# A four-layer residual kernel on TensorE: attention in eight places of the array, and a new order of the step

## The chip, the cores and the metric

The kernel runs on one core of one Trainium2 chip. The metric is the device time of one execution in microseconds (us). TensorE does the matrix products and turns (transposes), VectorE, ScalarE and GpSimd work elementwise, and SyncE issues the transfers. Inputs lie in device memory, tiles in SBUF, results of TensorE in eight PSUM banks of 512 fp32 columns.

## The reference

`x` has 64 sequences of 64 tokens of 512 values, fp32. Four layers follow each other, each added to its input:

```python
x = x + L0(x)   # x @ W.T + (x @ A[idx0].T) @ Bm[idx0].T * scal[idx0], rank 16, one of 8 adapters per sequence
x = x + L1(x)   # per sequence: weights[idx1].T (64x64) @ x (64x512), one of 200 matrices
x = x + L2(x)   # causal attention, 16 heads of 32, q scaled by min(cond, 4), scores / sqrt(32), then Wo
x = x + L3(x)   # as L1, with another table of 8 matrices and idx3
```

## The kernel before, in words

The 64 sequences go in 16 steps of four (256 tokens, two tiles of 128 tokens, two sequences in a tile). Every dense product with a 512x512 matrix is made from operands split in a high and a low part (`*_hi`, `*_lo`, type fp32r): high by high, high by low, low by high. Such a product is 24 matmuls of 512 columns a step (layer 0, values, output of attention) or 48 of 256 columns (keys, queries). The small products are plain fp32: mixing (layers 1 and 3, `mix`, L417, four matmuls in the four 64x64 quarters of the array), scores (L466) and attention (L485). In the trace an fp32 matmul of these three has two records, each with a weight load of its own; a turn has one.

Scores and attention use block-diagonal operands: `place_k`, `place_q`, `place_v` (L243, L249, L254) copy keys, queries and values out of PSUM into tiles with zeros in them, so that a 128x128 matmul makes the scores of two heads and two sequences at once, of which the zeros throw away the cross terms. `beta` scales the scores on VectorE (L802). Softmax goes: mask and maximum (VectorE), minus the maximum (GpSimd), exp (ScalarE), sum and reciprocal (VectorE), times the reciprocal (GpSimd for tile 0, VectorE for tile 1), then the turn of the probabilities on TensorE (L477).

The order on each engine is written out by hand in a function `step`, and engines meet through semaphores (`wait_ge`). TensorE's step i (L524) is: turn x of step i+1, queries, values of tile 0, scores, values of tile 1, the adapters' first product and layer 0 of step i+1, turns of the probabilities with the last of layer 0 between them, attention, the adapters' second product (`adapters_up`, L409), the output product of tile 0, layer 1 of step i+1, the output product of tile 1 with the turns of x1 inside it, keys of step i+1 with layer 3 of step i inside them. The low part of the adapters' intermediate (`xa_lo_part`, L771) has to be in place before `adapters_up`. SyncE's step (L328) gathers the per-sequence matrices, loads x two steps ahead and stores y. Before the loop the five 512x512 matrices are loaded one behind another on SyncE's queue, turned and split.

## Time and profile before

| | before |
|---|---|
| time of three runs, us | 713.11, 714.54, 714.82 (median 714.54) |
| the profiled execution: time, span, us | 714.74, 713.2 |
| busy: TensorE, VectorE, ScalarE, GpSimd | 96%, 53%, 45%, 16% |
| mean granted clock of TensorE | 0.988 |

The span runs from the first to the last instruction, the time is 1.5 us longer. "Busy" counts instructions in execution. Each duration of a matmul record holds a latency that overlaps its neighbours, so TensorE's rate is read from the starts of records, not from their durations. "PE" is TensorE, "PEld" its weight loads, "DVE" VectorE, "ACT" ScalarE, "POOL" GpSimd, "SPq" SyncE's queue, "L472" line 472.

### The profile page before, as it was taken

The page shows a single profiled execution, that of the slowest core. Times are in us where ns is not written, and L with a number is a line of the kernel's source. Part 1 is how long each engine was busy: PE and PEld are TensorE (multiplying, and loading weights), DVE is VectorE, ACT ScalarE, POOL GpSimd, SP SyncE. Part 2 cuts the span into 40 slices and gives each one's busy share as a digit, 9 for nine tenths or more (in the row PEclk, how much of TensorE's full clock was granted, in tenths as well). Part 3 has the DMA queues.
Part 4 walks back from the last instruction along what each step waited for, and adds up shares of the span by engine and source line. Part 5 has one row for each costly group of instructions (what it writes and reads, how often), then busy time and mean ns, then how long its engine had stood idle before and what let it go on. Part 6 is the DMA issues. An engine that isn't in the chain of part 4 may idle for free.

```text
span 713.2 us, 14872 instructions
## 1 busy us (share of the span) xinstructions
PE 683.2 (96%) x5240; PEld 584.7 (82%) x5240; DVE 378.9 (53%) x565; ACT 319.9 (45%) x648; POOL 113.9 (16%) x98
## 2 busy tenths in 40 slices
PE   5699999999999999999999999999999999999986
PEld 4489797888979798797979879797987979798774
DVE  3645555464555646455564645546463554636362
ACT  3544355443535544353554435354543535444342
POOL 4003012030301203030120303002030300303030
PEclk9979999999999999999999999999999999999998
DMA  6520111102011010201101020110202011020000
GB/s 185 191 94 8 53 37 35 49 4 81 7 52 37 33 52 4 81 7 52 37 30 54 5 81 7 52 37 18 65 5 81 7 52 37 9 75 4 29 1 30
DMA packets 32768, 31.68 MB, mean 44 GB/s; under 512 B 18550, under 2 KB 18550, under 8 KB 32758
## 3 DMA queue, kind: packets, MB, share of 16 engines
q1 hardware_dynamic: 32758, 31.55, 14.2%
q8 instruction: 6, 0.10, 0.1%
q14 instruction: 4, 0.03, 0.0%
HBM read 22.61 MB, written 8.91 MB: 44 GB/s over the span
## 4 chain that ended last, share of the span: by engine, by line
PE 92%; DMA 2%; DVE 2%; SPq 1%; issue 1%; ACT 0%; POOL 0%; ACTq 0%; DVEq 0%
PE banks L374 13%; PE banks L375 12%; PE banks L376 12%; PE banks L504 9%; PE banks L472 8%; PE banks L493 5%; PE banks L421 5%; PE banks L512 4%; PE banks L481 4%; PE banks L404 4%; PE banks L402 4%; PE banks L406 4%; PE banks L436 2%; PE banks L395 2%; PE banks L385 2%; PE banks L414 2%
## 5 line engine op out<-in xcount | busy, mean ns | idle before, releaser
L374 PE MATMUL banks<-x1T_hi,w_hi 128*128 128x256 f32 x512 | 148.3, 290 | 0.0
L375 PE MATMUL banks<-x1T_lo,w_hi 128*128 128x256 f32 x512 | 144.9, 283 | 0.0
L376 PE MATMUL banks<-x1T_hi,w_lo 128*128 128x256 f32 x512 | 144.8, 283 | 0.0
L374 PEld LDWEIGHTS banks<-x1T_hi,w_hi 128*128 128x128 f32 x512 | 98.1, 192 | 15.3 <-issue 15.3
L375 PEld LDWEIGHTS banks<-x1T_lo,w_hi 128*128 128x128 f32 x512 | 98.1, 192 | 0.0
L376 PEld LDWEIGHTS banks<-x1T_hi,w_lo 128*128 128x128 f32 x512 | 98.0, 191 | 0.0
L742 DVE COPY k_bd<-banks 32x512 f32<-32x512 f32 x64 | 44.2, 691 | 98.9 <-PE banks L376 98.2
L907 POOL TENSOR_TENSOR w_own<-w_in,own 128x128 f32<-128x128 f32 x32 | 14.7, 460 | 492.7 <-PE banks L421 287.0
L922 POOL TENSOR_TENSOR probs<-probs,row_max 128x1024 f32<-128x1024 f32 x32 | 61.0, 1907 | 84.2 <-DVE row_max L808 84.2
L677 ACT ACTIVATE probs<-probs 128x1024 f32<-128x1024 f32 x32 | 34.0, 1061 | 72.2 <-POOL probs L922 71.9
L802 DVE SCALAR_TENSOR_TENSOR probs<-banks,beta,mask 128x512 f32<-128x512 f32 x64 | 46.4, 747 | 37.2 <-PE banks L472 36.6
L472 PEld LDWEIGHTS banks<-k_bd,q_bd 128*128 128x128 f32 x512 | 59.5, 192 | 2.9 <-issue 1.8
L472 PE MATMUL banks<-k_bd,q_bd 128*128 128x128 f32 x512 | 59.8, 275 | 1.6 <-DVE q_bd L742 1.6
L605 ACT ACTIVATE v_bd<-banks 64x256 f32<-64x256 f32 x128 | 48.6, 379 | 24.8 <-PE banks L376 23.3
L812 DVE TENSOR_REDUCE row_sum<-probs 128x16 f32<-128x1024 f32 x32 | 39.0, 1220 | 38.7 <-ACT probs L677 38.7
L605 ACT ACTIVATE y<-banks 128x512 f32<-128x512 f32 x32 | 17.4, 597 | 84.8 <-PE banks L421 84.8
L504 PE MATMUL banks<-w_hi,attnT_hi 128*128 128x512 f32 x128 | 54.9, 429 | 0.0
L605 ACT ACTIVATE k_bd<-banks 32x512 f32<-32x512 f32 x64 | 37.6, 588 | 35.3 <-PE banks L376 34.8
L402 PE MATMUL banks<-w_hi,xT_hi 128*128 128x512 f32 x128 | 51.5, 402 | 0.0
L374 PE MATMUL banks<-w_hi,x1T_hi 128*128 128x512 f32 x128 | 51.4, 401 | 0.0
L504 PE MATMUL banks<-w_lo,attnT_hi 128*128 128x512 f32 x128 | 50.4, 394 | 0.0
L375 PE MATMUL banks<-w_lo,x1T_hi 128*128 128x512 f32 x128 | 50.1, 391 | 0.0
(93 smaller groups left out, 1222.5 us busy)
## 6 DMA issues: line engine op xcount, KB each, us to landing
x_in<-in_x_dram SPq DMA_DIRECT2D x16, 512.0 KB, 3.7
out_dram<-y SPq DMA_DIRECT2D x16, 512.0 KB, 2.8
b_sel<-b_parts SPq DMA_DIRECT2D x192, 32.0 KB, 1.8
w_in<-in_L_cond_weights_dram SPq DMA_DIRECT2D x128, 16.0 KB
probsT<-in_L_cond_W_dram SPq DMA_DIRECT2D x1, 1024.0 KB, 6.1
probs<-in_L_cond_Wk_dram SPq DMA_DIRECT2D x1, 1024.0 KB, 7.7
x_both<-in_L_cond_Wq_dram SPq DMA_DIRECT2D x1, 1024.0 KB, 10.0
probsT<-in_L_cond_Wv_dram SPq DMA_DIRECT2D x1, 1024.0 KB, 12.1
```

Source lines behind the costliest of these rows:

```text
L374: nc.tensor.matmul(out_ap, s_hi, m_hi, start=(k == 0), stop=False)
L375: nc.tensor.matmul(out_ap, s_hi, m_lo, start=False, stop=False)
L376: last = nc.tensor.matmul(out_ap, s_lo, m_hi, start=False, stop=(k == n - 1))
L402: nc.tensor.matmul(bank[3 + t][:], xT_hi[:, c, tok(t)], w_hi[:, W0, c, :], start=(c == 0), stop=False)
L421: nc.tensor.matmul(bank[first_bank + t][half(r ^ t), :], w_own[half(r), t, :], rows_of[half(r), t, :], start=True, stop=True).then_inc(don ...
L472: last = nc.tensor.matmul(bank[b][:, hp % 4 * P:(hp % 4 + 1) * P], q_bd[:, t, hp, :], k_bd[:, t, hp, :], start=True, stop=True)
L504: nc.tensor.matmul(bank[5 + t][:], attnT_hi[:, c, tok(t)], m[:, WO, c, :], start=(c == 0 and m is w_hi), stop=False)
L605: return nc.scalar.activation(dst, src, ACT.Copy)
L742: return nc.vector.tensor_copy(dst, src)
L802: last = nc.vector.scalar_tensor_tensor(out=heads(probs[:, t, n * BANK:(n + 1) * BANK]), in0=heads(bank[(5 + 2 * t + n) % 8][:]), scalar=b ...
L812: nc.vector.tensor_reduce(row_sum[:, t, :], heads(probs[:, t, :]), AX.X, ALU.add).then_inc(sum_done, 1)
L922: nc.gpsimd.tensor_tensor(heads(probs[:, t, :]), heads(probs[:, t, :]), rows[:, t, :].unsqueeze(2).to_broadcast([P, HEADS, S]), op).then_i ...
```

## The change

It rewrites the step; the dense products, their number and their sizes stay as they are.

- Scores: `k_bd`, `q_bd` and their copies go. Keys are copied as they lie (`kT`), queries are scaled by `beta` on their way out of PSUM (`scale_q`). Each head of each sequence is one matmul of 32 rows, 64 stationary and 64 moving columns, in one of eight places of the array (four groups of 32 rows, two halves of columns): 64 matmuls a step in place of 16. The scores of a step are ready all at once.
- Attention: `v_bd` and its copies go. Each head of each sequence is one matmul of 64 rows, 32 stationary and 64 moving columns, again in eight places: 64 matmuls a step in place of 32.
- Order: step i begins with the scores of step i, then the output product of step i-1, the adapters' first product and layer 0 of step i+1, `adapters_up`, turns of the probabilities around layer 3 of step i-1, layer 1 of step i+1, one tile's turn of x of step i+2, attention, the turns of x1 of step i+1, the other tile's turn of x, keys, queries, values of step i+1.
- The identity is added to the diagonal of W once, so x need not be added to layer 0's result; the copies of x0 and x1 are shared between ScalarE and VectorE; the copy `keep_x1` goes from ScalarE to GpSimd. x0 and y have tiles of their own.
- In the preparation the five matrices are loaded on ScalarE's queue, each to a buffer of its own; queries and values of step 0 are made before the loop; Wv is turned behind `adapters_up(0)` and Wo behind the queries.

```diff
-        k_bd = sb("k_bd", [P, TILES, HP, P])
...
+        qkT = sb("qkT", [P, 2, NC, PT])
+        qT = qkT[:, 0]
+        kT = qkT[:, 1]
+        v = sb("v", [P, TILES, D])
...
+        def in_steps(engine, step):
+            step(0)
+            with engine.Fori(1, LAST_ALIKE + 1) as i:
+                step(i)
+            for i in range(LAST_ALIKE + 1, PAIRS):
+                step(i)
...
+            def step(i):
+                if after(i, 2):
+                    gather_own_b(i + 2)
+                if after(i, -1):
+                    store_y(i - 1)
+                if after(i, 3):
+                    turned_in(i + 3)
+                if after(i, 1):
...
         @block.tensor
...
+            def scores(i):
+                pe.wait_ge(k_copied_act, i + 1)
+                pe.wait_ge(k_copied_dve, i + 1)
+                pe.wait_ge(q_scaled, TILES * (i + 1))
+                for mm in range(NC // 2):
+                    for t in range(TILES):
+                        for r in range(SEQT):
+                            for h in range(2):
+                                for j in range(JG):
+                                    m, rows = 2 * mm + h, slice(j * HD, (j + 1) * HD)
+                                    last = nc.tensor.matmul(bank[SC[j]][half(h), key_columns(m, t, r)],
+                                                            qT[rows, m, own_tokens(t, r)],
+                                                            kT[rows, m, own_tokens(t, r)], start=True, stop=True)
+                last.then_inc(s_mm, 1)
...
+            def attend():
+                for t in range(TILES):
+                    for m in range(NC):
+                        for r in range(SEQT):
+                            for j in range(JG):
+                                at = j % 2 * BANK + (m // 2 * TILES + t) * P + m % 2 * S
+                                head = (JG * m + j) * HD
+                                last = nc.tensor.matmul(
+                                    attn_bank(r)[j * HD:(j + 1) * HD, m, t, :], v[half(r), t, head:head + HD],
+                                    probsT[half(r), j // 2, at:at + S], start=True, stop=True)
+                last.then_inc(av_mm, 1)
...
-                for hp in range(HP):
-                    b = (5 + 2 * t + hp // 4) % 8
-                    last = nc.tensor.matmul(bank[b][:, hp % 4 * P:(hp % 4 + 1) * P], q_bd[:, t, hp, :],
-                                            k_bd[:, t, hp, :], start=True, stop=True)
-                    if hp % 4 == 3:
-                        last.then_inc(s_mm, 1)
...
-                for hp in range(HP):
-                    for b in range(SEQT):
-                        at = hp * P + b * S
-                        last = nc.tensor.matmul(
-                            bank[1 + t][half(hp % 2), hp // 2 * P + b * S:hp // 2 * P + (b + 1) * S],
-                            v_bd[:, t, b, hp, :], probsT[:, t, at:at + S], start=True, stop=True)
-                last.then_inc(av_mm, 1)
...
-            def step(i, more=True):
-                if more:
-                    turn_x(i + 1)
-                queries(i)
-                if more:
-                    values(0)
-                scores(i, 0)
-                if more:
-                    pe.wait_ge(xT_split, TILES * (i + 2))
-                scores(i, 1)
-                if not more:
-                    values(0)
-                values(1)
-                if more:
...
+            def step(i):
+                prev, nxt, nxt2 = after(i, -1), after(i, 1), after(i, 2)
+                scores(i)
+                if prev:
+                    for t in range(TILES):
+                        layer2_out(i - 1, t)
+                if nxt:
+                    if prev:
+                        pe.wait_ge(x2_added, TILES * (i - 1) + 1)
+                    else:
+                        pe.wait_ge(v_copied, 1)
                     adapters_down(i + 1)
-                    pe.wait_ge(v_placed, TILES * i + 1)
-                    layer0_dense(0)
-                    layer0_dense(1, range(NC - 1))
+                    layer0_dense()
+                    adapters_up(i + 1)
+                if prev:
+                    layer3_ready(i - 1)
+                if nxt:
+                    pe.wait_ge(xa_summed, i + 2)
                 turn_probs(i, 0)
-                if more:
-                    layer0_dense(1, [NC - 1])
+                if prev:
+                    layer3()
+                if nxt:
+                    layer1_ready(i + 1)
                 turn_probs(i, 1)
-                attend(i, 0)
-                if more:
-                    pe.wait_ge(xa_summed, i + 2)
-                attend(i, 1)
-                if more:
-                    adapters_up(i + 1)
-                layer2_out_hi(i, 0)
-                layer2_out_lo(i, 0, range(NC - 1))
-                if more:
-                    layer1_ready(i + 1)
-                layer2_out_lo(i, 0, [NC - 1])
-                if more:
+                if nxt:
                     layer1()
-                layer2_out_hi(i, 1, range(NC // 2))
-                if more:
-                    turn_x1(i + 1)
-                layer2_out_hi(i, 1, range(NC // 2, NC))
-                layer2_out_lo(i, 1)
-                if more:
-                    pe.wait_ge(x2_added, TILES * i + 1)
-                    keys(i + 1, [0])
-                layer3_ready(i)
-                if more:
-                    keys(i + 1, [1])
-                layer3()
-                if more:
-                    keys(i + 1, [2, 3])
...
+                pT_copied(i, HG)
+                if prev:
+                    pe.wait_ge(y_copied, TILES * i)
+                if nxt2:
+                    turn_x(i + 2, 0)
+                attend()
+                if nxt:
+                    turn_x1(i + 1, 0)
+                    turn_x1(i + 1, 1)
+                    if nxt2:
+                        turn_x(i + 2, 1)
+                    keys(i + 1)
+                    if nxt2:
+                        pe.wait_ge(xT_split, TILES * (i + 3))
+                    queries(i + 1)
+                    pe.wait_ge(attn_split, SEQT * (i + 1))
+                    values()
...
         @block.scalar
...
+            def step(i):
+                prev, nxt, nxt2 = after(i, -1), after(i, 1), after(i, 2)
+                if nxt:
                     select_a(i + 1)
...
+                    x0_copy(i + 1)
+                copy_pT(i, 0)
+                if prev:
+                    copy_y(i - 1)
+                copy_pT(i, 1)
+                if nxt:
                     x1_copy(i + 1)
                     x1T_hi_part(i + 1)
-                act.wait_ge(y_stored, 1 + 16 * i)
-                for t in range(TILES):
-                    act.wait_ge(y_mm, 1 + TILES * SEQT * i + SEQT * (t + 1))
-                    copy(y[:, t, :], bank[1 + t][:]).then_inc(y_copied, 1)
+                act.wait_ge(av_mm, i + 1)
+                copy(attn_of(attnT_hi[:], 0), attn_bank(0)).then_inc(attn_hi_done_act, 1)
+                if nxt2:
+                    for t in range(TILES):
+                        x_hi(i + 2, t)
+                if nxt:
+                    copy_k(i + 1)
+                    copy_v(i + 1)
...
         @block.vector
...
+            def scale_q(i):
+                for n in range(2):
+                    dve.wait_ge(q_mm, 2 * i + n + 1)
+                    nc.vector.tensor_tensor(
+                        qT[:, 2 * n:2 * n + 2, :].rearrange("p m (q s) -> p m q s", s=S),
+                        bank[SC[n]].rearrange("p (m q s) -> p m q s", m=2, s=S),
+                        beta[:, bass.ds(i * PSEQ, PSEQ)].unsqueeze(1).unsqueeze(3)
+                        .to_broadcast([P, 2, PSEQ, S]), ALU.mult).then_inc(q_scaled, 1)
...
+            def step(i):
+                prev, nxt, nxt2 = after(i, -1), after(i, 1), after(i, 2)
+                for g in range(HG):
+                    mask_and_max(i, g)
+                    if prev:
+                        add_x1(i - 1, g)
                 sums(i, 0)
+                if nxt:
+                    sum_xa(i + 1)
+                    scale_xa(i + 1)
                 sums(i, 1)
-                for t in range(TILES):
-                    dve.wait_ge(pT_mm, TILES * i + t + 1)
-                    copy(probsT[:, t, BANK:2 * BANK], bank[(6 + 2 * t) % 8][:]).then_inc(pT_copied_dve, 1)
-                    if more and t == 0:
-                        sum_xa(i + 1)
-                        scale_xa(i + 1)
-                if more:
+                if nxt:
                     xa_lo_part(i + 1)
-                for t in range(TILES):
-                    dve.wait_ge(attn_hi_done, TILES * i + t + 1)
-                    rest(attnT_lo[:, :, tok(t)], bank[1 + t][:].rearrange("p (c n) -> p c n", n=P),
-                         attnT_hi[:, :, tok(t)]).then_inc(attn_split, 1)
-                if more:
-                    add_x(i + 1)
-                add_x1(i, 0)
-                if more:
+                    x0_copy(i + 1)
+                for g in range(HG):
+                    copy_pT(i, g)
+                if nxt:
+                    x1_copy(i + 1)
                     x1T_lo_part(i + 1)
-                add_x1(i, 1)
+                dve.wait_ge(av_mm, i + 1)
+                copy(attn_of(attnT_hi[:], 1), attn_bank(1)).then_inc(attn_hi_done_dve, 1)
+                for r, done in enumerate((attn_hi_done_act, attn_hi_done_dve)):
+                    dve.wait_ge(done, i + 1)
+                    rest(attn_of(attnT_lo[:], r), attn_bank(r), attn_of(attnT_hi[:], r)).then_inc(attn_split, 1)
+                if nxt2:
+                    x_lo(i + 2)
+                if nxt:
+                    copy_k(i + 1)
+                    scale_q(i + 1)
...
         @block.gpsimd
...
+            def step(i):
+                for g in range(HG):
+                    pool.wait_ge(s_max, HG * i + g + 1)
+                    with_rows(ALU.subtract, g, row_max, s_less_max)
+                pool.wait_ge(inv_done, HG * i + 1)
+                keeps_x1(i)
+                with_rows(ALU.mult, 0, row_inv, probs_done[0])
+                keep_x1()
                 build_w3(i)
-                if more:
-                    build_w1(i + 1)
-                for t in range(TILES):
-                    pool.wait_ge(s_max, TILES * i + t + 1)
-                    with_rows(ALU.subtract, t, row_max, s_less_max)
-                pool.wait_ge(inv_done, TILES * i + 1)
-                with_rows(ALU.mult, 0, row_inv, probs_done[0])
+                if after(i, 2):
+                    build_w1(i + 2)
```

## Rows read from the trace of the kernel before

**Rows 1.** The page: span, busy time, share and instructions of each engine.

```profile
span 713.2 us, 14872 instructions
...
PE 683.2 (96%) x5240; PEld 584.7 (82%) x5240; DVE 378.9 (53%) x565; ACT 319.9 (45%) x648; POOL 113.9 (16%) x98
```

**Rows 2.** Window of one whole step (time, busy time by engine, clock, DMA).

```profile
351.76:393.49 41.73, 41.46 (x325) 35.55 (x324) 22.53 (x33) 19.10 (x39) 6.78 (x6) 1.00 0.12 38
```

**Rows 3.** Timeline of TensorE, one step's queries, values, scores: start, duration (us).

```profile
343.46 0.28 PE L374 MATMUL banks<-x1T_hi,w_hi 128*128 128x256 f32 x1
...
348.85 0.40 PE L374 MATMUL banks<-w_hi,x1T_hi 128*128 128x512 f32 x1
...
351.60 3.73 PE L472 MATMUL banks<-k_bd,q_bd 128*128 128x128 f32 x32
```

**Rows 4.** Chain that ended last, same step: start, length (us), what.

```profile
363.82 0.87 PE banks L481 x8
...
366.25 2.06 PE banks L493 x64
368.32 0.27 issue
368.59 0.70 PE banks L414 x2
...
372.24 1.02 PE banks L421 x8
```

**Rows 5.** Timeline at the start of a mixing product, window to 338.26.

```profile
338.23 0.15 PEld L421 LDWEIGHTS banks<-probs,w_own 64*64 64x64 f32 x4
338.24 0.66 PE L421 MATMUL banks<-probs,w_own 64*64 64x512 f32 x4
```

**Rows 6.** Windows near the end and of the preparation, columns as Rows 2.

```profile
35.90:44.20 8.30, 7.20 (x33) 5.58 (x34) 3.00 (x6) 4.08 (x7) 0.46 (x1) 0.50 0.48 157
...
697.72:700.85 3.13, 3.13 (x66) 3.06 (x65) 1.19 (x2) 1.19 (x2) 0.00 (x0) 0.63 0.00 0
```

**Rows 7.** Chain near the end: the last scores, softmax and attention.

```profile
681.88 0.13 PE banks L376
...
697.72 3.12 PE banks L493 x64
```

**Rows 8.** Groups of VectorE in one step: busy us, mean ns.

```profile
L802 DVE SCALAR_TENSOR_TENSOR probs<-banks,beta,mask 128x512 f32<-128x512 f32 x4 | 2.9, 746 | 2.4 <-PE banks L472 2.4
...
L808 DVE TENSOR_REDUCE row_max<-probs 128x16 f32<-128x1024 f32 x2 | 2.4, 1220 | 0.1
...
L796 DVE TENSOR_TENSOR probs<-banks,x_both 128x512 f32<-128x512 f32 x2 | 1.4, 692 | 1.2 <-PE banks L512 1.2
...
L817 DVE TENSOR_TENSOR probs<-probs,row_inv 128x1024 f32<-128x1024 f32 x1 | 1.2, 1228 | 0.0
L746 DVE TENSOR_TENSOR xa_parts<-xa,xa_hi 32x128 fp32r<-32x128 f32 x2 | 0.6, 282 | 0.2 <-ACT xa_hi L605 0.2
L814 DVE RECIPROCAL row_inv<-row_sum 128x16 f32<-128x16 f32 x2 | 0.5, 253 | 0.1
...
L761 DVE TENSOR_TENSOR xa_sum<-banks,xa_low 64x256 f32<-64x256 f32 x1 | 0.4, 406 | 0.0
```

**Rows 9.** Groups of ScalarE in the same step.

```profile
L677 ACT ACTIVATE probs<-probs 128x1024 f32<-128x1024 f32 x2 | 2.1, 1061 | 4.3 <-POOL probs L922 4.3
...
L605 ACT ACTIVATE x1T_hi<-banks 128x512 fp32r<-128x512 f32 x2 | 1.1, 596 | 0.5 <-PE banks L436 0.5
```

**Rows 10.** Groups of GpSimd in the same step.

```profile
L922 POOL TENSOR_TENSOR probs<-probs,row_max 128x1024 f32<-128x1024 f32 x2 | 3.8, 1906 | 4.3 <-DVE row_max L808 4.3
```

**Rows 11.** Timeline of TensorE in the preparation, waits in brackets.

```profile
34.16 1.02 PE L414 MATMUL banks<-b_sel,xa_parts 96*128 96x512 f32 x2 [3.51 <-DMA b_sel<-b_parts]
36.23 1.99 PE L421 MATMUL banks<-y,w_own 64*64 64x512 f32 x8 [1.04 <-DVE y L784]
...
40.72 3.62 PE L362 MATMUL banks<-ident,probs 128*128 128x128 f32 x16
```

More of the change, by code:

```diff
@@ new lines, in gather, with gather_b @@
+            def gather(dst, table, at, arrived, moved):
+                for n in range(PSEQ):
+                    t, b = divmod(n, SEQT)
+                    sp.dma_start(dst[half(b ^ t if moved else b), t, :],
+                                 table[bass.ds(at[n], 1), :, :].rearrange("a c e -> (a c) e")).then_inc(arrived, 16)
+            def gather_b(at):
+                for n in range(PSEQ):
+                    t, b = divmod(n, SEQT)
+                    for k, part in enumerate((0, 0, 1)):
+                        row = (k * SEQT + b) * RANK
+                        sp.dma_start(b_sel[row:row + RANK, t, :].bitcast(F32),
+                                     b_parts[part, bass.ds(at[n] * RANK, RANK), :]).then_inc(b_loaded, 16)
@@ new lines, in project_T @@
+            def project_T(w, out_banks, m, split=None):
+                out_ap = bank[out_banks[m // 2]][:, (m % 2) * PT:(m % 2 + 1) * PT]
+                cols = slice(m * P, (m + 1) * P)
+                for c in range(NC):
+                    nc.tensor.matmul(out_ap, w_hi[:, w, c, cols], x1T_hi[:, c, :], start=(c == 0), stop=False)
+                    nc.tensor.matmul(out_ap, w_lo[:, w, c, cols], x1T_hi[:, c, :], start=False, stop=False)
+                if split is not None:
+                    pe.wait_ge(x1_split, split)
+                for c in range(NC):
+                    last = nc.tensor.matmul(out_ap, w_hi[:, w, c, cols], x1T_lo[:, c, :], start=False,
+                                            stop=(c == NC - 1))
+                return last
@@ new lines, in keys, with queries, values @@
+            def keys(i):
+                pe.wait_ge(x1_hi_done, TILES * (i + 1))
+                for m in range(NC):
+                    last = project_T(WK, MIX, m, split=TILES * (i + 1) if m == 0 else None)
+                    if m % 2 == 1:
+                        last.then_inc(k_mm, 1)
+            def queries(i):
+                for m in range(NC):
+                    last = project_T(WQ, SC, m)
+                    if m % 2 == 1:
+                        last.then_inc(q_mm, 1)
+            def values():
@@ L593, in _ @@
-            turn_x1(0)
-            turn_matrix(4, groups_of(4)[0])
-            keys(0, range(NC))
-            pe.wait_ge(turned_lo, GROUPS)
-            with pe.Fori(0, PAIRS - 1) as i:
-                step(i)
-            step(PAIRS - 1, more=False)
+            turn_x1(0, 0)
+            turn_x1(0, 1)
+            keys(0)
+            pe.wait_ge(xT_split, TILES * 2)
+            queries(0)
+            turn_matrix(WO)
+            pe.wait_ge(turned_lo, GROUPS_OF[WV][-1] + 1)
+            values()
@@ L602, in _ @@
+            pe.wait_ge(turned_lo, GROUPS)
+            in_steps(pe, step)
+            for t in range(TILES):
+                layer2_out(PAIRS - 1, t)
+            layer3_ready(PAIRS - 1)
+            layer3()
         @block.scalar
@@ L952, in _ @@
                 nc.gpsimd.tensor_copy(mask[half(b), :], block_mask[half(b), half(b)]).then_inc(consts_step, 1)
[L953 to L954 removed]
+                pool.wait_ge(consts_step, 8 + 2 * b)
                 nc.gpsimd.tensor_copy(own[half(b), :], ident[half(b), half(b)]).then_inc(consts_step, 1)
[L956 to L958 removed]
+                pool.wait_ge(consts_step, 9 + 2 * b)
             build_w1(0)
[L960 to L962 removed]
+            build_w1(1)
+            in_steps(pool, step)
 _INS = ['x', 'itok_B_0_6', 'itok_B_1_198', 'cond_1', 'itok_B_0_7', 'L0_cond_W', 'L0_cond_A', 'L0_cond_Bm',
```

682 lines of the change are left out of this document (319 added, 363 removed).

## The prediction

> **What bounds the kernel.** I read the page first: TensorE is busy 96% of the span and no other engine much over half [rows 1]. Then a window of one whole step: 41.73 us, TensorE busy 41.46 of it at the full clock (1.00, 2.4 GHz), VectorE 22.5, ScalarE 19.1 [rows 2]. Each step in the middle takes this, so the kernel is TensorE's own rate, and a change is worth what it takes from TensorE's work or puts in as waits. Busy is not the rate, so I took the rate from starts. The 45 records of 256 columns between 343.46 and 348.85 follow each other at 0.120 us, the 12 of 512 columns between 348.85 and 351.60 at 0.229 [rows 3]; one of fp32 scores (16 matmuls of 128 columns, 32 records) takes 3.57/32 = 0.112, the scores ending near 355.17. One of attention (32 matmuls of 64 columns, 64 records) takes 2.06/64 = 32.2 ns [rows 4]. Last I read the chain at the end, where softmax has nothing to hide behind [rows 7], and the preparation [rows 11].
>
> **What stays.** Dense products, turns and mixings keep their number and sizes. In a step they are 96 records at 0.120 and 72 at 0.229, together 28.0; the adapters' first product 8 x 0.120 = 1.0 and the second about 0.5; 32 turns at 0.87 for eight, 3.5; two mixings at 1.02 [rows 4], 2.0. That is 35.0. With scores 3.57 and attention 2.06 it makes 40.7 of 41.73; the other 1.0 are the drains where the kind of product changes and one issue gap of 0.27 [rows 4]. The new order has about as many such changes, in fewer pieces: I take 1.0 again, the issue gap included. So the new step is 36.0 + S + A + new waits, S and A being the new scores and attention.
>
> **S and A, the disputed cost.** Each is 64 matmuls, so 128 records with weight loads, a record being 64 columns long, in eight places. Before shows no such stream; nothing keeps a cost from being anywhere between the ends of the nearest rows. Upper end: the pair (weight load and matmul) of attention at 32.2 ns gives 128 x 32.2 = 4.1 us each. Lower end: at the start of a mixing, four pairs in four quarters begin within 338.23 to 338.26 [rows 5], about 6.7 ns a pair: 0.86 us each. In between decides what the 32.2 consists of. The two column halves of attention alternate, so one place has a record each 64 ns; and the last attention, where the clock is 0.63 of full [rows 6], takes 3.12/64 = 48.8 ns a record [rows 7]. If a record costs a + b with only b following the clock, then b(1/0.63 - 1) = 16.6, b = 28.3 and a = 3.9 ns. b is the array's time over two places; over eight it is 28.3/4 = 7.1. So 11 ns a pair, 1.4 us each for S and A. I take that, being worked out from the very stream nearest in shape, and keep 0.86 and 4.1 for the range.
>
> The Trainium skill speaks against the change here: TensorE: Matmul & The Clock Gate, section "Wait — 56ns, not 53.3ns?", says that starts of matmuls never come closer than about 25 ns, however few the columns. By it S and A would be 3.2 us each, an estimate from that page, and the kernel slower. The burst of four pairs in some 30 ns [rows 5] disagrees, but it is short; no row shows a long stream. The number does not enter the sum.
>
> The copies around them (`k_bd`, `q_bd`, `v_bd`) go from VectorE and ScalarE; those engines are hidden behind TensorE, so this is worth nothing by itself, only slack: VectorE's new step is about as long, 22 us of some 40. Adding the identity to W costs four small additions in the preparation and spares nothing on TensorE. The shared copies of x0 and x1 shorten a link by half of 1.2 us.
>
> **New waits, with t = 0 at the end of the scores.** TensorE: output product of step i-1 to 5.6, adapters' first product to 6.6, layer 0 to 12.1, then `adapters_up`. VectorE: mask and maximum of group 0, 2 x 0.69 + 1.22 [rows 8], to 2.8; `add_x1` waits for the first output product, to 3.6; group 1 to 6.2; `add_x1` to 6.9. GpSimd's subtraction takes 1.91 [rows 10], 2.8 to 4.7 and 6.2 to 8.15; exp 1.06 [rows 9], to 5.8 and 9.3. VectorE's sum 1.22 and reciprocal 0.25 [rows 8] of group 0 end at 8.4; GpSimd multiplies to 10.4. VectorE goes on with the adapters' sum and scale (two operations near 0.41 [rows 8]) to 9.3, sums of group 1 to 10.9, the multiplication 1.23 to 12.2, and only behind these, in its queue, `xa_lo_part`, 2 x 0.28 [rows 8], to 12.9. So `adapters_up` waits about 0.9: what is queued behind it is everything on TensorE. The probabilities, ready at 10.4 and 12.2, are then early. Next: copies of the turned probabilities against layer 1, about 0.15 late (ScalarE copies y between them). Attention is what covers the copies of x1. The keys wait for the second `x1T_hi`, 0.6 each [rows 9], less the 0.45 of the turn of x: 0.4. Queries' scaling and copies of keys and values end under the values and the scores. SyncE: 12 gathers for `b_sel` from 13.5, then y's store, the x tile after both its turns (21), w3 and w1; each is used at least 10 us later, and costs nothing. If that cover failed the x tile would hold the first turn of the next step. Waits together 1.5.
>
> Step: 36.0 + 1.5 + 2 x 1.4 = 40.3. Taking the order's fewer pieces as 0.4 saved (dense blocks no longer cut by turns and mixings) I arrive at 39.9, a gain of 1.8 a step, over 15 steps 27.5 us.
>
> **Once only.** In step 0 no output product covers softmax: `xa_lo_part` ends near 12 and layer 0 near 6.6, so 4.5 more than the steady wait, and some 1 at the halved clock, as after the idle time near the end [rows 6]. Preparation: before, `adapters_up(0)` starts at 34.16 after waiting for `b_sel` [rows 11]; now five matrices share the transfers with it: 0 to 2 us later. Wv's 16 turns, once hidden before that wait, come behind it at the halved clock, 3.4 us by those of Wo [rows 11, 6]; the addition to x gives 0.6 back: together +4. At the end scores, softmax and output products follow as before (31.3 us from 681.88 to the end of the span [rows 7, 1]), with output product and layer 3 of step 14 as cover in place of the values: -1. Sum: 713.2 - 27.5 + 5.5 + 4 - 1 = 694.2 of span, 1.5 more as time. That profiled execution took 714.74 against the median 714.54, so the median forecast is **695.5 us**.
>
> **Rivals.** (a) Issue bound: the small pairs don't come closer than in attention before, 32.2 ns each. S + A rise by 5.4, and sixteen steps make 695 + 87 = 782 us. By the 25 ns of that page of the Trainium skill the same rival would end near 753, an estimate. For it: no long stream of eight places is in the trace. Against: rows 5, and that 32.2 follows the clock [rows 6, 7]. It decides from about 15.7 ns a pair, where 19 us are eaten over 16 x 256 pairs; places that don't work side by side, the change not doing what it says, end here too. (b) Eight places at the burst's rate: S = A = 0.86, 17 us less, 678. For it the burst [rows 5]; against it the part of 3.9 ns. (c) Softmax's chain is later than I add up: VectorE's queue holds `xa_lo_part` behind group 1, and each link that comes 1 us late is 1 us a step. With 1.5 more, 695 + 23 = 718, even or a little slower. For it: one long queue order without slack at `adapters_up`. Against: before's durations repeat within 1%.
>
> **Chances.** Forecast (685 to 705) 0.50; (b) or between, 0.17; (a) in full 0.12, and in part (16 to 30 ns) 0.06; (c) 0.15, of which half still ends below 712. Faster by over 0.3% (about what a measurement of this kernel can tell from no change): 0.50 + 0.17 + 0.09 = 0.76. Within: 0.04. Slower: 0.20. The range from 674 to 726 leaves out (a) in full and part of the rest; the likeliest case's own range is 685 to 705.
>
> **What would show it.** Right: records of scores and attention at 9 to 14 ns from start to start, each block 1.2 to 1.8 us; a step of 39.5 to 40.5; one wait of about 1 us before `adapters_up` that VectorE's `xa_lo_part` ends; a wait near 5 us in step 0. Wrong: starts at 16 ns or more; blocks over 2 us; a wait for x, for turned probabilities or for `x1T_hi` over 1 us a step; a clock below 1.00 in the middle.

## The result and the profile after

The changed kernel takes 733.37 us (median of four runs, 732.72 to 736.07) against 714.68 before: a ratio of 1.0274, 95% interval 1.0244 to 1.0303. It is slower by 2.7%, and the time lies above the range of the prediction. The profiled execution has a span of 731.8 us, 18.6 more than before.

The page after (span, busy time, granted clock in 40 slices), beside [rows 1]:

```profile
span 731.8 us, 19651 instructions
...
PE 650.8 (89%) x7800; PEld 545.1 (74%) x7800; DVE 371.7 (51%) x537; ACT 224.6 (31%) x440; POOL 127.2 (17%) x111
...
PEclk9779999999999999999999999999999999999998
```

TensorE works 32 us less than before (650.8 against 683.2) and the span is longer: more than what was saved came back as waits, in the preparation and in each step. Who TensorE waits for, in total, times, longest (us):

```profile
PE banks L403 <- DVE xa_parts L758: 30.2, 15, 4.7
PE banks L403 <- DMA b_sel<-b_parts: 9.4, 1, 9.4
PE banks L362 <- DMA v<-in_L_cond_Bm_dram: 9.0, 1, 9.0
PE banks L373 <- DMA x_in<-in_x_dram: 7.7, 1, 7.7
PE banks L434 <- ACT x1T_hi L618: 5.6, 16, 0.7
```

The first row is a wait of every step, before the adapters' second product (now L403), for VectorE's low part. The next three are the preparation. The timeline of TensorE in a middle step answers to [rows 3, 4]:

```profile
341.23 0.70 PE L403 MATMUL banks<-b_sel,xa_parts 96*128 96x512 f32 x2 [1.83 <-DVE xa_parts L758]
...
346.39 1.48 PE L502 MATMUL banks<-probsT,v 64*32 64x64 f32 x128
347.80 1.09 PE L425 MATMUL banks<-ident,x_both 128*128 128x128 f32 x8
...
349.63 0.38 PE L434 MATMUL banks<-x1T_hi,w_hi 128*128 128x256 f32 x1 [0.30 <-ACT x1T_hi L618]
...
366.80 1.59 PE L477 MATMUL banks<-qkT 32*64 32x64 f32 x128
368.32 0.50 PE L517 MATMUL banks<-w_hi,attnT_hi 128*128 128x512 f32 x1
```

The scores go from 366.80 to 368.32, 1.52 us for 128 records where 3.57 stood; attention from 346.39 to 347.80, 1.41 us where 2.06 stood. That is 11.9 and 11.0 ns a record. The waits in brackets are 1.83 us before the adapters' second product and 0.30 before the keys. The chain gives the starts of the scores of several steps:

```profile
118.17 1.52 PE banks L477 x91
...
160.98 1.52 PE banks L477 x91
...
325.69 1.52 PE banks L477 x91
...
366.87 1.52 PE banks L477 x91
```

A middle step is 366.87 - 325.69 = 41.18 us, 0.55 less than the 41.73 of [rows 2]; the one from 118.17 to 160.98 is 42.81, and one more like it begins at 490.40. The first scores begin at 77 us. Before, the same amount of work stood at 59.66 (scores) plus 2.75 (the values of tile 1), 62.4 us. So the account is: preparation +14.5, the rest of the span (731.8 - 77 against 713.2 - 62.4) +4. The experiments below are called e1 to e11; there is no e5.

### The profile page after: what moved, and what is told of

Its sections match the earlier page's. It is cut to its first block, busy times and chain, and to the rows that moved or that the text cites. A ratio compares the mean times of both kernels' runs of the same rounds, so it can differ in the third digit from the quotient of the medians.

```text
span 731.8 us, 19651 instructions
## 1 busy us (share of the span) xinstructions
PE 650.8 (89%) x7800; PEld 545.1 (74%) x7800; DVE 371.7 (51%) x537; ACT 224.6 (31%) x440; POOL 127.2 (17%) x111
## 4 chain that ended last, share of the span: by engine, by line
PE 65%; DVE 17%; issue 8%; SPq 5%; ACT 2%; POOL 1%; DMA 1%; DVEq 0%; ACTq 0%; POOLq 0%
PE banks L434 9%; PE banks L439 8%; PE banks L435 8%; PE banks L411 5%; DVE row_sum L832 5%; PE banks L487 5%; DVE xa L777 4%; PE banks L459 4%; PE banks L461 4%; PE banks L463 4%; PE banks L477 3%; PE banks L502 3%; DVE probs L823 3%; PE banks L517 3%; PE banks L524 2%
## 5 line engine op out<-in xcount | busy, mean ns | idle before, releaser
L434 PE MATMUL banks<-x1T_hi,w_hi 128*128 128x256 f32 x512 | 129.9, 286 | 5.6 <-ACT x1T_hi L618 5.6
L823 DVE TENSOR_TENSOR probs<-banks,mask 128x512 f32<-128x512 f32 x64 | 41.1, 684 | 100.1 <-PE banks L477 100.1
L439 PE MATMUL banks<-x1T_lo,w_hi 128*128 128x256 f32 x512 | 82.3, 283 | 0.0
L618 ACT ACTIVATE v<-banks 128x512 f32<-128x512 f32 x32 | 19.1, 598 | 197.9 <-PE banks L463 197.9
L439 PEld LDWEIGHTS banks<-x1T_lo,w_hi 128*128 128x128 f32 x512 | 70.6, 192 | 0.0
L814 DVE TENSOR_TENSOR qkT<-banks,beta 128x512 f32<-128x512 f32 x32 | 22.1, 692 | 70.0 <-PE banks L439 70.0
L393 PE MATMUL banks<-w_lo,xT_hi 128*128 128x512 f32 x128 | 50.5, 394 | 0.0
L395 PE MATMUL banks<-w_hi,xT_lo 128*128 128x512 f32 x128 | 50.2, 392 | 0.0
L463 PE MATMUL banks<-w_hi,x1T_lo 128*128 128x512 f32 x128 | 49.8, 389 | 0.0
L487 PEld LDWEIGHTS banks<-ident,probs 128*128 128x128 f32 x256 | 31.9, 152 | 21.4 <-issue 19.5
L403 PE MATMUL banks<-b_sel,xa_parts 96*128 96x512 f32 x32 | 12.2, 464 | 39.6 <-DVE xa_parts L758 30.2
```

The costliest lines, as they stand in the source:

```text
L434: nc.tensor.matmul(out_ap, w_hi[:, w, c, cols], x1T_hi[:, c, :], start=(c == 0), stop=False)
L439: last = nc.tensor.matmul(out_ap, w_hi[:, w, c, cols], x1T_lo[:, c, :], start=False, stop=(c == NC - 1))
L463: last = nc.tensor.matmul(bank[OUT[t]][:], x1T_lo[:, c, tok(t)], w_hi[:, WV, c, :], start=False, stop=(c == NC - 1))
L487: last = nc.tensor.transpose(bank[SC[2 * g + n]][:, c * P:(c + 1) * P], probs[:, g, at:at + P], ident[:])
L823: last = nc.vector.tensor_tensor(heads(probs[:, g, n * BANK:(n + 1) * BANK]), heads(bank[SC[2 * g + n]]), mask[:].unsqueeze(1).to_broadcas ...
```

## The wait in each step

Why does VectorE come late? Its timeline in that step, and GpSimd's under it:

```profile
335.31 0.35 DVE L771 TENSOR_TENSOR xa_sum<-banks,xa_low 64x256 f32<-64x256 f32 x1
335.81 1.99 DVE L777 TENSOR_TENSOR xa<-xa_sum,scal_rows 64x256 f32<-64x256 f32 x1
337.73 1.20 DVE L832 TENSOR_REDUCE row_sum<-probs 128x16 f32<-128x1024 f32 x1
...
339.25 1.23 DVE L837 TENSOR_TENSOR probs<-probs,row_inv 128x1024 f32<-128x1024 f32 x1
340.51 0.58 DVE L758 TENSOR_TENSOR xa_parts<-xa,xa_hi 32x128 fp32r<-32x128 f32 x2
```

```profile
335.62 1.91 POOL L963 TENSOR_TENSOR probs<-probs,row_inv 128x1024 f32<-128x1024 f32 x1 [0.25 <-DVE row_inv L834]
337.47 1.24 POOL L973 COPY x_both<-x_both 128x1024 f32<-128x1024 f32 x1
```

The scaling of the adapters' intermediate (L777) took 0.42 us before, as one of the two operations of [rows 8] near 0.41; now it lasts 1.99. It starts 0.19 us behind GpSimd's multiplication of the probabilities and ends 0.27 behind its end. Before, it stood behind the turns of the probabilities, when GpSimd was idle. The Trainium skill, SBUF — State Buffer, section "Who interferes with whom", says that VectorE and GpSimd share a pair of ports, that a VectorE instruction with two SBUF inputs and a GpSimd instruction that reads SBUF contend for it, that one of them holds it for the whole instruction while the other stands still, and that a VectorE instruction with at most one SBUF input, outside the modes that use both ports, does not contend. The scaling has two SBUF inputs (`xa_sum`, `scal_rows`); the mask (L823), with one input from PSUM and one from SBUF, takes 1.28 us beside GpSimd's subtraction in this step and 1.29 beside nothing. Theory 1 is this hold. Theory 2 is that the scaling is slow in itself where it now stands, and that only its place in the queue counts.

**e1, the sum kept in PSUM.** The scaling then has one SBUF input. Nothing is moved; TensorE's turns of the probabilities wait for the scaling in place of the sum, since the sum's place in PSUM is read until then.

```diff
-                    pe.wait_ge(xa_summed, i + 2)
+                    pe.wait_ge(xa_scaled, i + 2)
...
-                nc.vector.tensor_tensor(xa_sum[:], bank[OUT[0]][half(0), 0:PT], xa_low[:], ALU.add)\
-                    .then_inc(xa_summed, 1)
+                here = bank[OUT[0]][half(0), 0:PT]
+                nc.vector.tensor_tensor(here, here, xa_low[:], ALU.add).then_inc(xa_summed, 1)
...
-                    xa[:].rearrange("p (b s) -> p b s", s=S), xa_sum[:].rearrange("p (b s) -> p b s", s=S),
+                    xa[:].rearrange("p (b s) -> p b s", s=S),
+                    bank[OUT[0]][half(0), 0:PT].rearrange("p (b s) -> p b s", s=S),
```

> The changed kernel with one edit: VectorE's sum of the adapters' intermediate stays in PSUM, so that the scaling behind it has one SBUF input in place of two; nothing else is moved. Theory 1 (VectorE's two-input operation stands still while GpSimd multiplies the probabilities): the scaling falls from 1.99 to about 0.42 us. The multiplication of group 1 by VectorE, also with two SBUF inputs, then meets GpSimd's copy of x1 and may start only at its end, so the wait before the adapters' second product shrinks by 0.5 to 0.6 us a step (1.2 if that copy does not hold it): 733.4 goes to 722 to 725 (716). Theory 2 (the scaling is slow for another reason, its position or its data): it stays near 2 us and the time within 0.3% of 733.4.

Measured: 717.41 us, 1.0065 of before (1.0041 to 1.0089), 16.0 less than after (the spans, 731.8 and 715.8, differ by as much): a step is 0.90 less, 14 of them 12.6, and the two long steps are gone, 3.2. It is less than the 722 to 725 expected. VectorE, then GpSimd:

```profile
328.98 0.40 DVE L772 TENSOR_TENSOR banks<-banks,xa_low 64x256 f32<-64x256 f32 x1
329.52 0.42 DVE L777 TENSOR_TENSOR xa<-banks,scal_rows 64x256 f32<-64x256 f32 x1
...
331.70 1.55 DVE L838 TENSOR_TENSOR probs<-probs,row_inv 128x1024 f32<-128x1024 f32 x1
```

```profile
329.28 1.91 POOL L964 TENSOR_TENSOR probs<-probs,row_inv 128x1024 f32<-128x1024 f32 x1 [0.25 <-DVE row_inv L835]
331.13 1.04 POOL L974 COPY x_both<-x_both 128x1024 f32<-128x1024 f32 x1
```

The scaling is back at 0.42 us in the midst of GpSimd's multiplication: Theory 1 holds, Theory 2 falls. The multiplication of group 1, with two SBUF inputs, begins while GpSimd copies x1 and takes 1.55 in place of 1.23, so that copy holds it too, by 0.3 us; I had expected 0.7. GpSimd pays as well: its copy lasts 1.04 here and 1.24 after, where it begins while the scaling still runs. A middle step is 40.28 us. The wait before the adapters' second product is 0.93 us a step (17.0 us in total less the 4.0 of step 0, over 14), the 0.9 that the prediction had.

**e2, the low part ahead of the multiplication.** Only the place in the queue changes.

```diff
                 nc.vector.reciprocal(row_inv[:, g, :], row_sum[:, g, :]).then_inc(inv_done, 1)
                 if g == 1:
+                    if after(i, 1):
+                        xa_lo_part(i + 1)
...
                 sums(i, 1)
                 if nxt:
-                    xa_lo_part(i + 1)
                     x0_copy(i + 1)
```

> The changed kernel with VectorE's low part of the adapters' intermediate placed ahead of its multiplication of group 1, the scaling left as it is. Theory 1 and the order in the queue: the scaling stays at 1.99 us, the low part is in place 1.3 us sooner, the wait before the adapters' second product shrinks from 1.8 to about 0.5 us: 733.4 goes to about 714. A rival (that wait is of the high part on ScalarE, which hangs on the same scaling): the wait shrinks by less than 0.5 us, 728 or more.

Measured: 712.65 us, 0.9998 of before (0.9981 to 1.0014), a step of 39.91 us. The order of the queue is worth 1.27 us a step, more than the 0.90 of the hold. Neither alone ends the wait: 0.93 us of 1.83 are left in e1, 0.55 here.

**e3, both edits.**

> The changed kernel with both edits. Theory 1: no wait before the adapters' second product in the middle steps; 1.8 us in 14 steps and the two steps of 42.8 us back at the others' length: 733.4 goes to 704 to 708, a middle step takes 39.3 us. Rival (the next link, copies of x0 or the probabilities, is as late): a new wait of 0.5 to 1 us in its place, 712 to 720.

Measured: 700.34 us, 0.9834 of before (0.9813 to 0.9854). Chain, starts of the scores:

```profile
350.37 1.52 PE banks L477 x91
...
389.48 1.52 PE banks L477 x91
```

A step is 39.11 us, and in it TensorE waits for nothing but the copies of the turned x1, 0.3 us. The wait before the adapters' second product stands only in step 0, 2.8 us in place of 4.7. No step of 42.8 is left. Sum against the trace after: 14 x 2.06, 3.1 in step 0 and 3.2 in the two long steps make 35.1; the spans differ by 731.8 - 696.6 = 35.2. Those two edits alone, with the preparation as it was, make the rewrite faster than before.

**e9, GpSimd's multiplication cut in two.** How long does the hold last?

```diff
-                with_rows(ALU.mult, 0, row_inv, probs_done[0])
+                for n in range(2):
+                    half_row = slice(n * BANK, (n + 1) * BANK)
+                    last = nc.gpsimd.tensor_tensor(
+                        heads(probs[:, 0, half_row]), heads(probs[:, 0, half_row]),
+                        row_inv[:, 0, n * HEADS // 2:(n + 1) * HEADS // 2].unsqueeze(2)
+                        .to_broadcast([P, HEADS // 2, S]), ALU.mult)
+                last.then_inc(probs_done[0], 1)
```

> The changed kernel with GpSimd's multiplication of group 0 cut into two instructions of half the width, nothing else. If VectorE's two-input operation stands still until GpSimd's running instruction ends, the scaling falls from 1.99 to about 1.3 us and the middle step from 41.18 to 40.5. If both merely share a rate while both run, it stays near 2 us. If it waits for GpSimd's whole queue of work, the copy of x1 included, it would be above 2 us.

Measured, in a single run: 721.18 us. The views of the scaling's line and of GpSimd's (durations in ns: least, median, most):

```profile
L777 DVE TENSOR_TENSOR xa<-xa_sum,scal_rows x16: 416/1128/1130, 35.7 to 655.7; 64x256 f32<-64x256 f32 x16
...
L983 POOL TENSOR_TENSOR probs<-probs,row_inv x32: 1043/1048/1230, 85.6 to 696.5; 128x512 f32<-128x512 f32 x32
```

1.13 us in place of 1.99, and 0.416 where GpSimd does nothing, in the preparation; a middle step is 40.61 us. VectorE waits for the end of GpSimd's running instruction, not for its whole work and not at a shared rate: the scaling ends 0.27 us behind the end of the first half, as it did behind the end of the whole. In its turn it holds GpSimd: the second half takes 1.23 us in place of 1.05 in every step but the last, where nothing is scaled. That agrees with the rule of the Trainium skill cited above (SBUF — State Buffer, "Who interferes with whom").

## The preparation

SyncE's queue after, at the start:

```profile
1.94 14.88 SPq L295 DMA_DIRECT2D v<-in_L_cond_Bm_dram  x4
16.86 3.29 SPq L297 DMA_DIRECT2D idx_row<-in_itok_B_dram  x1
...
24.76 7.39 SPq L271 DMA_DIRECT2D w_in<-in_L_cond_weights_dram  x8
...
35.93 0.65 SPq L313 DMA_DIRECT2D b_parts<-b_lo  x1
38.55 11.46 SPq L280 DMA_DIRECT2D b_sel<-b_parts  x16
```

The four loads of B, many small pieces, take 14.88 us to issue; before the change they took 6.12 with W alone of the five matrices ahead of them. Now five matrices sit on ScalarE's queue beside them. Then come eight gathers of w1 and w3 in the same queue, 7.4 us, ahead of `b_parts` and the gathers for `b_sel`, and the adapters' second product of step 0 starts at 46.80 in place of 34.16 [rows 11]. So 12.6 of the preparation's 14.5 us stand ahead of it. Of these 3.0 are another wait: x lands 6.6 us after its issue in place of 3.5, and TensorE's first turn, which waits for it, starts at 7.66 us where before it started at 4.70. No experiment removes that wait; it is 7.4 to 7.8 us in all of them.

**e4, A and B ahead of four matrices.**

```diff
                 act.dma_start(stage[k], matrix.rearrange("(c p) d -> p c d", p=P)).then_inc(w_loaded[k], 16)
+                if k == W0:
+                    act.wait_ge(ab_loaded, 16 * AB_DMAS)
```

> The changed kernel with one edit in the preparation: ScalarE's queue loads W at once and the other four matrices only when A and B have landed. Theory (the four loads of B, 16.9 us to issue and land behind five matrices that share the transfer engines, set the start of everything through b_parts and b_sel): the four issues take 6 us again as before the change, the second product of step 0 starts at 36 us in place of 46.8, and 733.4 goes to about 722. Rival (the matrices themselves are then late: Wk and Wq land some 8 us later and their turns wait): less than 3 us gained.

Measured: 726.08 us, 1.0175 of before (1.0132 to 1.0218). SyncE's queue and TensorE:

```profile
1.94 7.64 SPq L295 DMA_DIRECT2D v<-in_L_cond_Bm_dram  x4
```

```profile
38.55 1.06 PE L403 MATMUL banks<-b_sel,xa_parts 96*128 96x512 f32 x2 [2.33 <-ACT xa_parts L618]
...
68.68 1.59 PE L477 MATMUL banks<-qkT 32*64 32x64 f32 x128
```

The four issues take 7.64 us, the second product starts at 38.55 and the first scores at 68.68, 8.2 sooner than after, of which the medians show 7.3. My 11 missed that the wait stands ahead of ScalarE's copies of W, which are now late by 7 us.

**e7, the step's edits with three of the preparation.** Beside the wait just shown, the gathers for layer 3 go behind those of `b_sel`, and `turn_matrix(WV)` with its copies goes ahead of `adapters_up(0)`.

> Both edits of the step (sum in PSUM, low part ahead of the multiplication) and three of the preparation: A and B ahead of the four matrices, the gathers for layer 3 behind those of b_sel, and Wv turned ahead of the adapters' second product of step 0. Theory: the step of 39.1 us, and the first scores at 60 to 62 us in place of 77: 700.3 (both edits of the step alone) less 15 to 17, 683 to 686 us. Rival (the transfers bound the preparation whatever their order, some 7.5 MB): first scores no sooner than 68, 692 or more.

Measured: 690.08 us, 0.9674 of before (0.9637 to 0.9712). The first scores start at 68.1 (66.5 in the next run, whose preparation is the same): neither the 60 to 62 of the theory nor, with 690, quite the rival's 692. The first scores of e4 start at 68.7, so the gathers and Wv, moved together, gained next to nothing beyond it.

**e8, the last step.** The additions of x1 go behind both maxima where no step follows.

> As the run before, and in the last step both additions of x1 stand behind both maxima in VectorE's queue, so that GpSimd's second subtraction doesn't wait for the output product of step 14. Expected: 1 us less at the end, hardly more than the measurement tells; if the softmax chain of the last step is bound by GpSimd's three operations in any order, no change.

Measured: 688.69 us, 0.9656 of before (0.9621 to 0.9692). The interval overlaps the run before. GpSimd's second subtraction starts 1.2 us sooner, but the turns of the probabilities only 0.3 (TensorE's wait went from 4.6 to 4.3 us), and from the last scores to the end it is 33.6 us in both traces: the edit gained nothing that shows. It is the best version here by its median, not shown to be better than e7 or e10.

What makes the end long shows in the chains, first before, then after:

```profile
683.58 2.04 PE banks L472 x16
...
696.15 1.57 PE banks L481 x8
```

```profile
697.17 1.54 PE banks L477 x91
...
709.08 1.94 PE banks L487 x8
711.02 1.64 PE banks L411 x8
...
717.99 0.50 PE banks L517
```

From the last scores to the turns of the probabilities in the chain it is 11.9 us after (697.17 to 709.08), less than the 12.6 before (683.58 to 696.15). From there to the output product it is 8.9 us (to 717.99), where before had 4.7: the turn's 1.57 and attention's 3.12 [rows 7]. Layer 3 of step 14 (L411), meant as cover for softmax, stands between the two turns and delays attention by 1.6; TensorE waits 0.8 for the copies of the turned probabilities and 2.0 for attention's low part. The turns in the chain take 1.4 more than the one of before, attention 1.6 less.

**e10, W's copies first, layer 0 ahead of A and B.**

```diff
-            pe.wait_ge(ab_loaded, 16 * AB_DMAS)
-            turn(GROUP_A, [a_nat[:, c * P:(c + 1) * P] for c in range(NC)])
-            turn(GROUP_B, [b_nat[:, c, :] for c in range(NC)])
             pe.wait_ge(turned_lo, NC)
             pe.wait_ge(xT_split, TILES)
             layer0_dense()
+            pe.wait_ge(ab_loaded, 16 * AB_DMAS)
+            turn(GROUP_A, [a_nat[:, c * P:(c + 1) * P] for c in range(NC)])
+            turn(GROUP_B, [b_nat[:, c, :] for c in range(NC)])
             adapters_down(0)
...
+            act.wait_ge(ab_loaded, 16 * AB_DMAS)
+            for k, matrix in ((WK, Wk), (WQ, Wq), (WV, Wv), (WO, Wo)):
+                load_matrix(k, matrix)
             take_hi(GROUP_A, a_all[:, :, 0, :], in_chunks(bank_of_group(GROUP_A)))
```

> As e8_mended_end, with two more edits of the preparation: ScalarE issues the four matrices behind its copies of W instead of waiting for A and B ahead of them (that wait held W's copies up by 7 us in e4, e7 and e8), and TensorE makes layer 0 of step 0 before it turns A and B. Theory: the 6.7 to 7.6 us for which TensorE waits on W's low parts go, first scores at 60 to 62 us in place of 66.5, 688.7 goes to 683 to 685. Rival (the other matrices or b_sel are then the late ones, being issued later): a wait on a transfer of 3 us or more appears and less than 2 us are gained.

Measured: 689.45 us, 0.9663 of before (0.9634 to 0.9691): no gain, the first scores at 67.5, and the expectation was wrong. The waits of TensorE show where it went:

```profile
PE banks L383 <- ACT a_sel L617: 4.2, 1, 4.2
PE banks L362 <- DVE w_lo L762: 4.1, 3, 2.4
```

Of the 12.6 us for low parts of the matrices in e8, 6.0 are left (the 4.1 shown and 1.9 before layer 0), but the selection of A now waits behind the late turn of A (4.2), and no transfer is waited for after x. The preparation is a chain through all engines. It stays at 67 us, 5 more than before; 3 of these are the wait for x, the rest stays open.

## The small products and the order of the step

**e6, the scores one place after another.** Loops exchanged, so that eight neighbours share a place.

```diff
-                for mm in range(NC // 2):
-                    for t in range(TILES):
-                        for r in range(SEQT):
-                            for h in range(2):
-                                for j in range(JG):
+                for h in range(2):
+                    for j in range(JG):
+                        for mm in range(NC // 2):
+                            for t in range(TILES):
+                                for r in range(SEQT):
```

> The changed kernel with the scores' 64 matmuls in another order: all eight of one place behind one another, then those of the next place, so that neighbours share a place. Theory (a place takes about 57 ns of array time per record of 64 columns, and eight places share it): 128 records at about 60 ns, 7.7 us for the scores in place of 1.52, 6 us a step more, 830 us. Rival (the 11.9 ns are an issue rate, whatever the place): the scores stay at 1.5 us and the time at 733.

Measured, in a single run: 867.49 us. The chain:

```profile
76.42 7.88 PE banks L477 x128
...
124.48 8.09 PE banks L477 x128
```

7.9 and 8.1 us for 128 records, 62 ns each on average. But the windows within one of these blocks (behind the counts: granted clock, DMA share, GB/s) show that the average mixes two clocks:

```profile
124.48:127.00 2.52, 2.52 (x54) 2.52 (x54) 0.00 (x0) 1.39 (x4) 0.00 (x0) 1.00 0.00 0
127.00:130.00 3.00, 3.00 (x56) 3.00 (x52) 0.00 (x0) 0.44 (x2) 0.00 (x0) 0.75 0.00 0
130.00:132.50 2.50, 2.50 (x28) 2.38 (x26) 0.00 (x0) 0.00 (x0) 0.00 (x0) 0.50 0.02 7
```

At 1.00 it is 2.52/54 = 47 ns a record, at 0.50 (1.2 GHz) 2.50/28 = 89 (records cut by an edge of a window are counted in it). These are averages over changes of place. The starts of the trace's single records lie 58 to 59 ns apart within a place at the full clock, 106 to 107 at the halved one, and 4 to 6 at some changes of place. TensorE is busy throughout and the clock falls all the same, while it works in one place; it stays down behind the scores, where the records of 512 columns follow each other at 0.43 us instead of 0.23:

```profile
133.30 0.43 PE banks L519
```

So the 11.9 ns of the change are eight places at work side by side, as the prediction said, and its price for one place, 3.9 + 56.6 = 60.5 ns, was near. Its split was not: with a + b = 58 and a + 2b = 107, a is 9 and b 49, and a + b/8 gives 15 for eight places, where 11.0 to 11.9 were measured. What sets these is not shown; in the streams of the change most single starts lie up to 17 ns apart, with a gap of some 60 here and there. The step, 48.1 to 50.7 us in place of 41.2, pays 4.5 for the records at the full clock (128 x (47 - 11.9)), some 2 for the clock within the scores, and the rest, up to 3, behind them. I had compared one place only by its time, and not foreseen the clock.

**e11, attention behind the turns of x1.**

```diff
                 if nxt2:
                     turn_x(i + 2, 0)
-                attend()
                 if nxt:
                     turn_x1(i + 1, 0)
                     turn_x1(i + 1, 1)
                     if nxt2:
                         turn_x(i + 2, 1)
+                attend()
+                if nxt:
                     keys(i + 1)
```

> The changed kernel with attention behind the turns of x1 and x instead of ahead of them, nothing else. Theory: attention is cover either way, for the copies of x1 (0.7 us) ahead of the turns or for the copies of the turned x1 behind them; the wait of 0.3 us before the keys goes and one of about 0.3 us before the first turn of x1 comes, and a middle step stays within 0.2 us of 41.18. Rival (the place of attention matters as the change's description has it): a middle step 0.5 us longer or more.

Measured, in a single run: 731.73 us. Chain:

```profile
324.22 1.52 PE banks L477 x91
...
365.25 1.52 PE banks L477 x91
```

41.03 us against 41.18: moving attention gains 0.15 us a step, so its place in the change is no help. The 0.3 before the keys became a wait of much the same size before the turns of x1.

## Why the prediction was wrong, by its own steps

- **What bounds the kernel; what stays.** Right. 41.18 - 1.83 - 0.30 - 1.52 - 1.41 leaves 36.1 us for all that stays; the prediction had 36.0.
- **S and A.** Right: 1.52 and 1.41 against 1.4 each. Rival (a) does not occur. The Trainium skill's floor of some 25 ns between starts (TensorE: Matmul & The Clock Gate, section "Wait — 56ns, not 53.3ns?") does not hold across places: 11 to 12 ns in streams of 128. e6 shows the mechanism, that the places work side by side: 47 ns at the same clock when they don't. That the sum came so near to 11 ns is partly luck, since its fixed part of 3.9 and its division by places don't fit e6's records.
- **New waits.** This step failed. "Two operations near 0.41 to 9.3" took the scaling's duration from a place where GpSimd was idle and set it beside GpSimd's multiplication, which the same paragraph had put at 8.4 to 10.4. It lasted 1.99, `xa_lo_part` came 0.9 later than summed, and the wait was 1.83 in place of 0.9. With the scaling back at 0.42 the wait is 0.93 (e1). That is rival (c), with a mechanism I had not named; it had 0.15. Experiments e1, e2, e3 and e9 show it.
- **The 0.4 for fewer pieces.** Not found. With it and the 0.9 the step is 41.2 in place of 39.9: 18 us over 14 steps.
- **Once only, preparation.** This failed as well: +4 said, +14.5 measured. "Five matrices share the transfers: 0 to 2 us later" priced the landing and not the issue; the four loads of B held SyncE's queue for 14.9 us, and the eight gathers behind them, 7.4 us, were passed over. e4 shows the first, worth 8 us of start; moving four of the gathers, with Wv, added next to nothing (e7). x, which the prediction left where it was, landed 3.0 us later.
- **Step 0 and the end.** Step 0 took 41.2 us where the sum had 38.8 (39.9 less 6.6 for the products it lacks, plus 4.5 and the 1 for the clock); with both edits of the step it takes 38.0 (e3), so this miss is the same chain. The end took 34.6 us from the last scores where 30.3 was said (31.3 less 1). "Output product and layer 3 of step 14 as cover" failed: layer 3 covers nothing where it stands, and the copies and the split around attention are waited for, 4.2 us more between the first turn and the output product.
- **The clock in the middle.** Two steps of 42.8, 3.2 us in all, were not foreseen (last section).

The misses add up: steps 17.9, less 0.7 for the last of them, which turns no x; preparation 10.5, clock 3.2, step 0 2.4, end 4.3. Together they are 37.6, and the span was 731.8 against 694.2 forecast. The forecast gain per step was there to be had: e3, which leaves the preparation as it was, takes 700.34 us, within the 685 to 705 of the likeliest case.

## What to carry to other kernels

When an operation moves to another place in a queue, its duration goes along only if its neighbours do: look at what GpSimd does at that time, and count the SBUF inputs of the VectorE operation. Keeping one sum in PSUM, at the price of waiting for another semaphore, took some 16 us out here (733.37 to 717.41). Work that others wait for goes ahead in a queue of work that nobody waits for: moving the low part ahead of one multiplication took 20.7 (733.37 to 712.65). Small products are worth laying out over the places of the array so that neighbours in the stream differ in place (733.37 against 867.49). What is meant as cover has to stand ahead of what waits, not between its parts. And a load moved to another queue changes how long the loads of many pieces take to issue, with everything queued behind them.

## What the runs showed of the hardware

The granted clock fell in the middle of the kernel in two steps, each time behind the wait of 1.83 us. Two windows of the trace after, each from the adapters' second product to the turn of x (last columns: granted clock, DMA share, GB/s):

```profile
133.60:139.98 6.38, 6.26 (x35) 3.29 (x36) 2.08 (x3) 2.88 (x5) 0.46 (x1) 0.73 0.18 46
341.20:345.80 4.60, 4.57 (x34) 2.51 (x34) 2.08 (x3) 2.79 (x5) 0.46 (x1) 1.00 0.15 42
```

The same work took 6.4 us at a mean clock of 0.73 (at 0.50, the lower of the two levels, for a part of it) in the step from 118.17, against 4.6 us at 1.00 in the step from 325.69. TensorE had waited 2 us and then turned probabilities. It happened in 2 of 14 steps after and in 2 of e4, both with that wait of 1.83; in none of e11, whose wait is 1.8 too; and in none where the wait is shorter: 1.26 us in e9, 0.93 and less in e1, e2 and e3. So the wait is not enough by itself, that it is the cause is not shown, and why it was those steps is open.

An fp32 stream in eight places runs at 11 to 12 ns a record of 64 columns. In one place records start 58 ns apart at the full clock and 107 at the halved one, and with neighbours in one place the clock fell some 4 us into the scores although TensorE never paused (e6). VectorE's operations with an operand in PSUM ran at full speed beside GpSimd (the scaling in e1 0.42 us, the mask 1.28). The same scaling with two SBUF inputs took 1.99, 1.13 and 0.42 us beside a whole, a half and no instruction of GpSimd, and GpSimd's next instruction lost some 0.2 us to it (1.24 for 1.04, and 1.23 for 1.05).
